# Two graph-attention layers on one core: the first pairs and the last pairs in another order, and one wait of VectorE per scores group in place of four

## The chip, the cores and the metric

The kernel runs on one core of a Trainium2 chip. Its engines are TensorE (PE, matrix products into PSUM), VectorE (DVE), ScalarE (ACT), GpSimd (POOL) and SyncE (SP, which here issues all DMAs). Each works through its own list of instructions in order, and they meet through semaphores. The metric is the device time of one execution in microseconds (us). Before the change it was 2106.66 us, the median of three runs (2102.52, 2106.66 and 2108.08).

## What is computed

128 graphs of 128 nodes with 384 features pass through two attention layers with 12 heads of 32. Cut to what matters:

```python
# layer 0: queries and keys without bias, bias on v, an output projection
q, k, v = x @ Wq.T, x @ Wk.T, x @ Wv.T + bv            # split into 12 heads
s = einsum('bqhd,bkhd->bhqk', q, k) * 384 ** -0.5 + 2 * adj
p = softmax(where(any(s != 0, -1), s, -inf)); p = nan_to_num(p)
x = layernorm(x + (p @ v) @ Wo.T + bo)
# layer 1: biases on q, k and v, no output projection
q, k, v = x @ Wq + bq, x @ Wk + bk, x @ Wv + bv
s = q @ k.T / sqrt(32) + beta * adj
p = softmax(where(adj > 0, s, -9e15))
x = layernorm(x + p @ v)
```

All tensors are f32. The projections are made as three products of a high and a low part each.

## The kernel before

The 128 graphs are worked on in 64 pairs. The rows, queries and keys of a pair are made together (256 columns); scores, softmax, values and norms are made per graph, g = 0 or 1. A step has the form `step(layer, pair, g)`. For one graph and one layer the steps follow one another like this:

- PE `transpose_x` / `transpose_x1`, then ACT `high_xT` / `high_x1T` and DVE `low_xT` / `low_x1T` (L1147), which split the transposed rows in two parts.
- PE `project_qk` j = 0 to 5 (nine products of 256 columns each, L408 to L410) and `project_v` (nine of 384), each taken out of its PSUM bank by ACT `qk_out` (L761 to L765), DVE `values_out0` (L1202) or ACT `values_out1`.
- PE `scores` (L458): 12 heads into four banks, three heads to a bank. DVE `negate` (L1125): 12 instructions that add the adjacency, write the negated scores and their minimum. ACT `exps` (L807): 12 exponentials with their sums, in slices `exps(layer, pair, g, first, end)`.
- Layer 0: POOL `fold_scores0`, DVE `abs_max` and `inverse_sums0` (L1174 to L1213), POOL `normalise0` (L1515). Layer 1: DVE `inverse_sums1` (L1183).
- DVE `flip_probs` (L1141) transposes inside blocks of 32 into the tile `flip` (layer 0) or `stage` (layer 1). SP `spread_probs` (L292) moves the blocks by four DMAs into `prob0T` or `prob1T`, which PE `attend` (L474) multiplies with the values.
- Layer 0: ACT `high_o0T`, DVE `low_o0T` (L1147), PE `project_out0`, DVE `add_residual0` (L1093), norm. Layer 1: ACT `out1T_out`, PE `transpose_out1`, DVE `attention_out1` (L1191), POOL `residual1` (L1507), norm, SP `store` (L260).

There is one tile for the probabilities of a layer, so the exponentials of a layer's next graph wait for the flip of the one before (`flip_done`), and a flip waits until the blocks of the one before have landed (`probT_loaded`). The sums of layer 1 stand in one tile too: its exponentials also wait for `inverse_sums1` of the graph before (`inv1_done`). `attention_out1(q, g)` waits for the store of the pair before with the same g, since both use y. Four PSUM banks go round among all other products (`RING_USERS`), so that a step often waits for the reader of an unrelated one.

Each engine's order is written out by hand. `iterations` (L98) runs `first()`, then `body` for pairs 3 to 7, then a loop over pairs 8 to 61 with two bodies in a turn, then `last()`. In one body five or six pairs are under way at different stages. In `first()` the pairs are called q0, q1, q2, ... from the start; in `last()` z0 is the last pair, z1 the one before it, and so on.

## Time and profile before

| | us |
|---|---|
| median of three runs | 2106.66 |
| the profiled execution, its own time | 2102.98 |
| its span, from the first to the last instruction | 2101.1 |
| PE busy | 2033.8 (97%) |
| ACT busy | 1884.3 (90%) |
| DVE busy | 1813.3 (86%) |
| POOL busy | 1644.0 (78%) |

The profile shows one execution on the chip. PE, DVE, ACT and POOL are the engines, PEld is PE's loading of weights, SPq is SyncE's issue of DMAs. A row of the timeline has the start in us from the span's start, the duration in us, engine, line and operation, output<-input, how many were merged, and, in brackets, how long the engine was idle before it and what released it. The granted clock of PE (PEclk) is a share of 2.4 GHz: 1.00 is 2.4 GHz, 0.50 is 1.2 GHz.

### The profile page before, as it was taken

The page shows a single profiled execution, that of the slowest core. Times are in us where ns is not written, and L with a number is a line of the kernel's source. Part 1 is how long each engine was busy: PE and PEld are TensorE (multiplying, and loading weights), DVE is VectorE, ACT ScalarE, POOL GpSimd, SP SyncE. Part 2 cuts the span into 40 slices and gives each one's busy share as a digit, 9 for nine tenths or more (in the row PEclk, how much of TensorE's full clock was granted, in tenths as well). Part 3 has the DMA queues.
Part 4 walks back from the last instruction along what each step waited for, and adds up shares of the span by engine and source line. Part 5 has one row for each costly group of instructions (what it writes and reads, how often), then busy time and mean ns, then how long its engine had stood idle before and what let it go on. Part 6 is the DMA issues. An engine that isn't in the chain of part 4 may idle for free.

```text
span 2101.1 us, 85420 instructions
## 1 busy us (share of the span) xinstructions
PE 2033.8 (97%) x23808; PEld 1910.1 (91%) x23808; DVE 1813.3 (86%) x8324; ACT 1884.3 (90%) x7816; POOL 1644.0 (78%) x2187
## 2 busy tenths in 40 slices
PE   6899999999999999999999999999999999999984
PEld 5799989999999999999999999999999999999974
DVE  4688889988989989888889888889889889888885
ACT  4699989999999999999999999999999999999885
POOL 3677878888888888888888888888888888788874
PEclk9999999999999999999999999999999999999997
DMA  4345555555555555555555555555555555555554
GB/s 147 73 107 134 136 134 127 140 134 125 141 134 126 140 134 128 138 134 129 137 134 129 137 134 131 135 134 132 134 134 136 130 134 136 130 134 137 122 125 109
DMA packets 225441, 274.22 MB, mean 131 GB/s; under 512 B 25680, under 2 KB 225360, under 8 KB 225360
## 3 DMA queue, kind: packets, MB, share of 16 engines
q1 hardware_dynamic: 225360, 273.26, 54.2%
q8 instruction: 36, 0.59, 0.1%
q14 instruction: 45, 0.37, 0.1%
HBM read 46.67 MB, written 25.17 MB: 34 GB/s over the span
## 4 chain that ended last, share of the span: by engine, by line
POOL 56%; issue 27%; PE 5%; POOLq 3%; DVE 3%; DMA 3%; SPq 2%; ACT 1%; DVEq 0%; ACTq 0%
POOL prob L1515 12%; POOL flip L1488 10%; POOL norm L1449 6%; POOL x_late L1500 5%; POOL y L1507 4%; POOL x_bo L1465 4%; POOL adj L1478 4%; POOL mask L1476 3%; POOL flip L1491 3%; POOL norm L1446 2%; DMA prob0T<-flip 2%; SPq L292 2%; POOL norm L1453 1%; PE r_bank L408 1%; PE r_bank L409 1%
## 5 line engine op out<-in xcount | busy, mean ns | idle before, releaser
L807 ACT ACTIVATE prob<-neg_s,heads 128x128 f32<-128x128 f32 x3072 | 1190.7, 393 | 17.7 <-DVE flip L1141 7.9
L807 ACT ACTIVATION_READ_ACCUMULATOR prob<-neg_s,heads 128x1 f32 x3072 | 591.6, 193 | 0.0
L1515 POOL TENSOR_TENSOR prob<-prob,heads 128x512 f32<-128x512 f32 x384 | 389.2, 1042 | 92.4 <-DVE heads L1213 92.4
L408 PE MATMUL r_bank<-xT_hi,w_hi 128*128 128x256 f32 x1152 | 356.4, 309 | 16.0 <-DVE xT_lo L1147 9.7
L1488 POOL TENSOR_TENSOR flip<-neg_s 128x768 f32<-128x768 f32 x128 | 236.0, 1843 | 169.1 <-DMA prob0T<-flip 161.5
L1125 DVE CUSTOM_DVE_ANT_0 neg_s<-s_bank,bias 128x128 f32<-128x128 f32 x1536 | 333.5, 286 | 18.9 <-PE s_bank L458 12.1
L1125 DVE CUSTOM_DVE_ANT_0 neg_s<-s_bank,adj 128x128 f32<-128x128 f32 x1536 | 333.5, 285 | 6.8 <-PE s_bank L458 6.7
L408 PE MATMUL r_bank<-x1T_hi,w_hi 128*128 128x256 f32 x1152 | 330.3, 287 | 3.5 <-DVE x1T_lo L1147 1.6
L410 PE MATMUL r_bank<-xT_hi,w_lo 128*128 128x256 f32 x1152 | 327.0, 284 | 0.0
L409 PE MATMUL r_bank<-xT_lo,w_hi 128*128 128x256 f32 x1152 | 326.8, 284 | 0.0
L409 PE MATMUL r_bank<-x1T_lo,w_hi 128*128 128x256 f32 x1152 | 324.2, 281 | 0.0
L410 PE MATMUL r_bank<-x1T_hi,w_lo 128*128 128x256 f32 x1152 | 323.8, 281 | 0.0
L408 PEld LDWEIGHTS r_bank<-xT_hi,w_hi 128*128 128x128 f32 x1152 | 218.8, 190 | 44.4 <-DVE xT_lo L1147 10.3
L1125 DVE DVE_READ_ACCUMULATOR2_ANT heads<- 128x1 f32 x3072 | 255.3, 83 | 0.0
L1141 DVE STREAM_TRANSPOSE flip<-prob 128x1536 f32<-128x1536 f32 x128 | 227.6, 1778 | 31.9 <-POOL prob L1515 30.4
L1141 DVE STREAM_TRANSPOSE stage<-prob 128x1536 f32<-128x1536 f32 x128 | 225.6, 1762 | 3.1 <-DMA prob1T<-stage 2.6
L408 PEld LDWEIGHTS r_bank<-x1T_hi,w_hi 128*128 128x128 f32 x1152 | 217.0, 188 | 5.5 <-issue 2.0
L409 PEld LDWEIGHTS r_bank<-xT_lo,w_hi 128*128 128x128 f32 x1152 | 219.9, 191 | 0.0
L410 PEld LDWEIGHTS r_bank<-xT_hi,w_lo 128*128 128x128 f32 x1152 | 219.3, 190 | 0.0
L409 PEld LDWEIGHTS r_bank<-x1T_lo,w_hi 128*128 128x128 f32 x1152 | 217.2, 189 | 0.0
L410 PEld LDWEIGHTS r_bank<-x1T_hi,w_lo 128*128 128x128 f32 x1152 | 216.7, 188 | 0.0
L1449 POOL TENSOR_TENSOR norm<-norm,neg_half 128x1 f32<-128x1 f32 x256 | 144.1, 563 | 21.3
(85 smaller groups left out, 5472.2 us busy)
## 6 DMA issues: line engine op xcount, KB each, us to landing
prob0T<-flip SPq DMA_DIRECT2D x512, 192.0 KB, 3.6
prob1T<-stage SPq DMA_DIRECT2D x512, 192.0 KB, 3.6
x_in<-in_x_dram SPq DMA_DIRECT2D x128, 192.0 KB, 3.3
out_dram<-y SPq DMA_DIRECT2D x128, 192.0 KB, 2.7
adj<-in_adj_dram SPq DMA_DIRECT2D x256, 64.0 KB, 2.7
prob<-in_L_gnn_Wq_dram SPq DMA_DIRECT2D x1, 576.0 KB, 4.5
prob0T<-in_L_gnn_Wk_dram SPq DMA_DIRECT2D x1, 576.0 KB, 5.7
stage<-in_L_gnn_Wv_dram SPq DMA_DIRECT2D x1, 576.0 KB, 7.8
```

Of the source, the lines that this page charges most:

```text
L408: pe.matmul(dst, a_hi(c), b_hi(c), start=(c == 0), stop=False)
L409: pe.matmul(dst, a_hi(c), b_lo(c), start=False, stop=False)
L410: mm = pe.matmul(dst, a_lo(c), b_hi(c), start=False, stop=(c == C - 1))
L807: act.activation(prob[layer][:, h, :], neg_s[layer][:, h, :], ACT.Exp, bias=neg_max[layer][:, h:h + 1], scale=-1.0, accum_out=row_sum[laye ...
L1125: dve.tensor_tensor_reduce(neg_s[layer][:, h, :], s_bank[b][:, (h // HC) * N:(h // HC + 1) * N], (adj0, bias1)[layer][q.parity][:, g, :], ...
L1141: dve.transpose(flip[layer].rearrange("p (j h b) -> p h j b", j=NB, h=H), prob[layer][:].rearrange("p h (j a) -> p h j a", j=NB)).then_inc ...
L1449: pool.tensor_tensor(rstd[layer][g][:], var_eps[layer][g][:], neg_half[:], ALU.pow).then_inc(rstd_steps[layer], 1)
L1465: pool.tensor_tensor(x_bo[b][:, g, :], x_in[b][:, g, :], bo_row[:], ALU.add).then_inc(x_bo_done, 1)
L1478: pool.tensor_scalar(adj1[:, g, :], adj1[:, g, :], 0.0, beta_col[:], ALU.max, ALU.mult).then_inc(bias1_steps, 1)
L1488: pool.tensor_tensor(fold_a, neg_s[0][:, :, 0:N // 2], neg_s[0][:, :, N // 2:N], ALU.add).then_inc(fold_steps, 1)
L1500: pool.tensor_tensor(x1_late[q.parity][:, g, :], x1[q.parity][:, g, :], bv_row[1][:], ALU.add).then_inc(late_done, 1)
L1515: pool.tensor_tensor(prob[0][:, hs, :], prob[0][:, hs, :], inv_sum0[:, hs].unsqueeze(2).to_broadcast([P, HC, N]), ALU.mult).then_inc(probn ...
```

## The change

The change has two parts. Nothing is computed otherwise than before.

The first part is one signal and one wait per scores group. PE raised `s_done` on each of the last four of the twelve head products, one for each bank, and DVE waited once for each bank. Now PE raises it on the last product alone, and DVE waits once ahead of the twelve instructions. ACT's `qk_out` waits for the same point as before.

```diff
@@ scores
-                        if c == C - 1:
-                            mm.then_inc(s_done[layer], 1)
+                    mm.then_inc(s_done[layer], 1)
@@ qk_out
-                    act.wait_ge(s_done[layer], q.plus(-2).count(HC, 1, HC))
+                    act.wait_ge(s_done[layer], q.plus(-2).count(1, 1, 1))
@@ negate
                             dve.wait_ge(exp_done[layer], q.count(H, g, 0))
-                        dve.wait_ge(s_done[layer], q.count(HC, g, b + 1))
-                        dve.sem_inc(dve_passed, 1)
+                            dve.wait_ge(s_done[layer], q.count(1, g, 1))
+                            dve.sem_inc(dve_passed, 1)
```

The second part is the order in `first()` and in `last()` on all five engines. `body`, and with it pairs 3 to 7 and the loop, keeps its order on each engine. A few of the lines:

```diff
@@ first, SP
+                load_adj0(q1)
                 load_x(q1)
-                load_adj0(q1)
+                load_adj1(q0)
@@ first, ACT
                 high_weights(WK0)
-                high_weights(WV0)
                 qk_out(0, q0, 0, 0)
+                high_weights(WO0)
@@ first, DVE
                 values_out0(q0, 0)
-                low_weights(WO0)
@@ last, PE
-                scores(1, z1, 1, LOOP_N)
                 project_qk(1, z0, 0, LOOP_N)
                 project_qk(1, z0, 1, LOOP_N)
-                transpose_out1(z2, 0, LOOP_N)
                 project_qk(1, z0, 2, LOOP_N)
+                scores(1, z1, 1, LOOP_N)
@@ last, SP
+                spread_probs(1, z2, 0)
                 store(z4, 1)
-                spread_probs(1, z2, 0)
+                store(z3, 0)
                 spread_probs(1, z2, 1)
-                store(z3, 0)
                 load_adj1(z0)
+                store(z3, 1)
                 spread_probs(1, z1, 0)
-                store(z3, 1)
                 store(z2, 0)
...
```

In DVE's part the line numbers are lower by five in the changed kernel (L1147 becomes L1142, L1141 becomes L1136).

The first place is DVE at the start of the program, right behind the twelve `negate` instructions of q0's graph 0. Before, the rows are these:

```order
L1202 TENSOR_TENSOR v_0<-r_bank,bv_row 128x384
L1084 TENSOR_TENSOR w_lo<-stage,w_hi 128x1152
L1202 TENSOR_TENSOR v_0<-r_bank,bv_row 128x384
L1174 TENSOR_REDUCE heads<-flip 128x12
L1176 SCALAR_TENSOR_TENSOR heads<-heads 128x12
L1209 RECIPROCAL heads<-heads 128x12
L1213 SCALAR_TENSOR_TENSOR heads<-heads 128x12
L1125 ISA neg_s,heads<-s_bank,adj_0 128x128
L1125 ISA heads 128x1
```

The same place in the changed kernel:

```order
L1197 TENSOR_TENSOR v_0<-r_bank,bv_row 128x384 x2
L1169 TENSOR_REDUCE heads<-flip 128x12
L1171 SCALAR_TENSOR_TENSOR heads<-heads 128x12
L1204 RECIPROCAL heads<-heads 128x12
L1208 SCALAR_TENSOR_TENSOR heads<-heads 128x12
L1142 TENSOR_TENSOR xT_lo<-r_bank,xT_hi 128x3x128 x2
L1136 STREAM_TRANSPOSE flip<-prob 128x12x4x32
L1120 ISA neg_s,heads<-s_bank,adj_0 128x128
L1120 ISA heads 128x1
```

The low part of the weight WO0 (L1084) has gone to a later place. The two low parts of q1's rows and the flip of q0's graph 0, which stood behind the twelve `negate` instructions of graph 1, stand ahead of them.

The second place is DVE in `last()`, around layer 1's graph 0 of z3. Before, these rows follow the flip of that graph, one L1191 and the twelve instructions of graph 1's `negate`, of which the last is the first row here:

```order
L1125 ISA heads 128x1
L1174 TENSOR_REDUCE heads<-flip 128x12
L1176 SCALAR_TENSOR_TENSOR heads<-heads 128x12
L1209 RECIPROCAL heads<-heads 128x12
L1213 SCALAR_TENSOR_TENSOR heads<-heads 128x12
L1147 TENSOR_TENSOR o0T_lo<-r_bank,o0T_hi 128x384
L1183 RECIPROCAL heads<-heads 128x12
L1103 BN_STATS norm_0<-y_0 128x6
```

In the changed kernel the flip itself (`stage<-prob`) is the second row, and the `negate` of graph 1 begins with the last:

```order
L1186 TENSOR_TENSOR y_0<-r_bank,heads 128x384
L1136 STREAM_TRANSPOSE stage<-prob 128x12x4x32
L1178 RECIPROCAL heads<-heads 128x12
L1088 TENSOR_TENSOR y_0<-r_bank,x_bo 128x384
L1098 BN_STATS norm_0<-y_0 128x6
L1101 BN_AGGR norm_0<-norm_0 128x2
L1120 ISA neg_s,heads<-s_bank,bias_0 128x128
```

Layer 1's reciprocal (L1183, now L1178) has moved from behind `negate`, the four instructions of layer 0's sums and a low part to the place right behind its flip.

The third place is SP near the end. `prob1T<-stage` is a spread of layer 1, `out_dram<-y_0` and `out_dram<-y_1` are stores of a graph 0 and a graph 1. Before, from the spread of z0's layer 0 graph 1 on (the x8 are both graphs of z2, the stores behind them are z3's graph 0, z3's graph 1 and z2's graph 0):

```order
L292 DMA prob0T<-flip 128x1x384 x4
L260 DMA out_dram<-y_1 32x4x384
L292 DMA prob1T<-stage 128x1x384 x8
L260 DMA out_dram<-y_0 32x4x384
L254 DMA adj<-in_adj_dram 128x1x128 x2
L292 DMA prob1T<-stage 128x1x384 x4
L260 DMA out_dram<-y_1 32x4x384
L260 DMA out_dram<-y_0 32x4x384
L292 DMA prob1T<-stage 128x1x384 x4
```

The same stretch in the changed kernel:

```order
L292 DMA prob0T<-flip 128x1x384 x4
L292 DMA prob1T<-stage 128x1x384 x4
L260 DMA out_dram<-y_1 32x4x384
L260 DMA out_dram<-y_0 32x4x384
L292 DMA prob1T<-stage 128x1x384 x4
L254 DMA adj<-in_adj_dram 128x1x128 x2
L260 DMA out_dram<-y_1 32x4x384
L292 DMA prob1T<-stage 128x1x384 x4
L260 DMA out_dram<-y_0 32x4x384
L292 DMA prob1T<-stage 128x1x384 x4
```

The stores of z3 each stand one spread earlier: graph 0's ahead of the spread of z2's graph 1, and graph 1's ahead of the spread of z1's graph 0.

## Rows read from the trace of the kernel before

**Rows 1.** Busy time by stretch (stretch: length, busy us per engine, PEclk, DMA share, GB/s).

```profile
0.00:30.00 30.00, 16.64 (x132) 14.61 (x132) 13.79 (x47) 15.17 (x39) 6.28 (x12) 1.00 0.60 193
30.00:40.00 10.00, 4.56 (x21) 4.59 (x22) 4.18 (x17) 2.75 (x12) 5.46 (x7) 0.54 0.50 117
40.00:110.00 70.00, 60.52 (x616) 55.32 (x615) 40.48 (x178) 43.70 (x168) 45.38 (x46) 0.99 0.28 66
110.00:300.00 190.00, 187.07 (x2193) 175.40 (x2192) 165.16 (x773) 172.21 (x727) 146.83 (x193) 1.00 0.55 127
300.00:1900.00 1600.00, 1600.00 (x18890) 1510.82 (x18890) 1437.34 (x6622) 1488.76 (x6212) 1299.88 (x1733) 1.00 0.56 134
1900.00:2000.00 100.00, 97.10 (x1168) 90.72 (x1166) 86.37 (x398) 89.76 (x377) 81.57 (x107) 1.00 0.52 123
2000.00:2101.00 101.00, 67.89 (x798) 58.68 (x798) 66.03 (x296) 71.92 (x289) 58.56 (x96) 0.86 0.50 121
```

**Rows 2.** Timeline of PE in the loop, scores groups.

```profile
612.79 0.95 PE L458 MATMUL s_bank<-k0T,q0T 32*128 32x128 f32 x24
622.45 0.95 PE L458 MATMUL s_bank<-k1T,q1T 32*128 32x128 f32 x24
644.23 0.95 PE L458 MATMUL s_bank<-k0T,q0T 32*128 32x128 f32 x24
```

**Rows 3.** Timeline of DVE in the loop, the first `negate` instruction of a group.

```profile
623.57 0.29 DVE L1125 CUSTOM_DVE_ANT_0 neg_s<-s_bank,bias 128x128 f32<-128x128 f32 x1 [0.16 <-PE s_bank L458]
```

**Rows 4.** Timeline of DVE at the start: a weight's low part, then three flips.

```profile
23.60 2.74 DVE L1084 TENSOR_TENSOR w_lo<-stage,w_hi 128x1152 fp32r<-128x1152 f32 x1
31.58 1.78 DVE L1141 STREAM_TRANSPOSE flip<-prob 128x1536 f32<-128x1536 f32 x1 [0.18 <-POOL prob L1515]
48.85 1.78 DVE L1141 STREAM_TRANSPOSE flip<-prob 128x1536 f32<-128x1536 f32 x1 [1.62 <-POOL prob L1515]
94.25 1.78 DVE L1141 STREAM_TRANSPOSE flip<-prob 128x1536 f32<-128x1536 f32 x1
```

**Rows 5.** Timeline of PE at the start, q1's first product.

```profile
35.44 0.55 PE L408 MATMUL r_bank<-xT_hi,w_hi 128*128 128x256 f32 x1 [6.65 <-DVE xT_lo L1147]
```

**Rows 6.** The page's groups: operation, count | busy us, mean ns | idle.

```profile
L807 ACT ACTIVATE prob<-neg_s,heads 128x128 f32<-128x128 f32 x3072 | 1190.7, 393 | 17.7 <-DVE flip L1141 7.9
```

**Rows 7.** Timeline of DVE and ACT in `last()`, around z3.

```profile
2006.18 1.77 DVE L1141 STREAM_TRANSPOSE stage<-prob 128x1536 f32<-128x1536 f32 x1
...
2013.83 0.22 DVE L1183 RECIPROCAL heads<-heads 128x12 f32<-128x12 f32 x1
...
2014.13 0.40 ACT L807 ACTIVATE prob<-neg_s,heads 128x128 f32<-128x128 f32 x1 [2.41 <-DVE heads L1183]
```

**Rows 8.** Timeline of DVE near the end: L1141 flips, L1191 readings of attended values.

```profile
2047.29 1.78 DVE L1141 STREAM_TRANSPOSE stage<-prob 128x1536 f32<-128x1536 f32 x1 [0.66 <-DMA prob1T<-stage]
...
2056.65 0.56 DVE L1191 TENSOR_TENSOR y<-r_bank,heads 128x384 f32<-128x384 f32 x1 [4.05 <-DMA out_dram<-y]
...
2065.88 0.56 DVE L1191 TENSOR_TENSOR y<-r_bank,heads 128x384 f32<-128x384 f32 x1 [3.60 <-DMA out_dram<-y]
2066.35 1.77 DVE L1141 STREAM_TRANSPOSE stage<-prob 128x1536 f32<-128x1536 f32 x1
...
2075.03 1.78 DVE L1141 STREAM_TRANSPOSE stage<-prob 128x1536 f32<-128x1536 f32 x1 [0.38 <-ACT prob L807]
...
2082.63 1.78 DVE L1141 STREAM_TRANSPOSE stage<-prob 128x1536 f32<-128x1536 f32 x1 [1.92 <-DMA prob1T<-stage]
```

**Rows 9.** Timeline of SP near the end: spreads and stores.

```profile
2058.92 3.07 SPq L292 DMA_DIRECT2D prob1T<-stage  x4
2062.04 3.91 SPq L260 DMA_DIRECT2D out_dram<-y  x2
...
2076.84 2.90 SPq L292 DMA_DIRECT2D prob1T<-stage  x4
```

**Rows 10.** Timeline of ACT near the end, z0's first exponential of layer 1.

```profile
2070.27 0.40 ACT L807 ACTIVATE prob<-neg_s,heads 128x128 f32<-128x128 f32 x1 [1.72 <-DVE heads L1125]
```

**Rows 11.** Timeline of PE, the last two attends.

```profile
2082.66 1.50 PE L474 MATMUL r_bank<-prob1T,v 128*32 128x128 f32 x24 [4.07 <-DMA prob1T<-stage]
...
2090.43 1.50 PE L474 MATMUL r_bank<-prob1T,v 128*32 128x128 f32 x24 [4.70 <-DMA prob1T<-stage]
```

More of the change, by code:

```diff
@@ L637, in last @@
-                scores(1, z3, 0, LOOP_N)
-                transpose_x1(z2, 0, LOOP_N)
-                project_v(1, z3, 1, LOOP_N)
-                project_v(0, z0, 1, LOOP_N)
-                project_qk(0, z0, 4, LOOP_N)
+                transpose_x1(z2, 1, LOOP_N)
                 project_qk(0, z0, 5, LOOP_N)
-                transpose_x1(z2, 1, LOOP_N)
+                attend(0, z1, 0, LOOP_N)
                 attend(1, z4, 0, LOOP_N)
-                attend(0, z1, 0, LOOP_N)
+                scores(0, z0, 0, LOOP_N)
@@ L663, in last @@
-                attend(1, z3, 0, LOOP_N)
                 project_v(1, z2, 1, LOOP_N)
                 transpose_x1(z1, 0, LOOP_N)
+                scores(1, z2, 0, LOOP_N)
                 transpose_x1(z1, 1, LOOP_N)
                 attend(0, z0, 0, LOOP_N)
-                scores(1, z2, 1, LOOP_N)
+                attend(1, z3, 0, LOOP_N)
+                transpose_out1(z3, 0, LOOP_N)
+                project_out0(z0, 0, LOOP_N)
                 project_qk(1, z1, 0, LOOP_N)
-                project_out0(z0, 0, LOOP_N)
@@ L1018, in last @@
[L1018 removed]
+                high_o0T(z0, 0)
+                out1T_out(z3, 0)
                 exps(0, z0, 1, 10, 12)
[L1020 to L1024 removed]
+                exps(1, z2, 0, 0, 8)
                 qk_out(1, z1, 0, LOOP_N)
[L1026 removed]
                 qk_out(1, z1, 1, LOOP_N)
+                exps(1, z2, 0, 8, 12)
@@ L1581, in last @@
                 inverse_std(0, z2, 1)
+                fold_scores0(z1, 1)
+                inverse_std(1, z5, 0)
+                normalise0(z1, 1)
+                inverse_std(1, z5, 1)
                 make_bias1(z3, 1)
-                fold_scores0(z1, 1)
-                late_x1(z3, 0)
-                normalise0(z1, 1)
-                inverse_std(1, z5, 0)
-                inverse_std(1, z5, 1)
+                residual1(z4, 0)
+                late_x1(z3, 1)
+                inverse_std(1, z4, 0)
```

452 lines of the change are left out of this document (223 added, 229 removed).

## The prediction

> **What bounds the kernel now.** I read the busy time by stretch first. The reader is to see one number in each row, the length less PE's busy time: 13.4 us without work in the first 30, then 5.4, 9.5 and 2.9 up to 300; 0 in the 1600 us from 300 to 1900; 2.9 and 33.1 in the last two stretches [rows 1]. Between 300 and 1900 PE is busy throughout at 2.4 GHz and a pair returns after 644.23 - 612.79 = 31.44 us [rows 2]. `body` keeps its order, so nothing is to be won there unless PE's own work shrinks, and the change moves no product. Only the 31.2 us of PE's idle time at the start and the 36.0 at the end are open. In both, PE is not what binds. There are two chains of VectorE, ScalarE, GpSimd and the spreads, one per layer: exponentials, flip, spread, next flip. I read these from the flips [rows 4, 8].
>
> **One wait per scores group.** The group that starts at 622.45 lasts 0.95, to 623.40, and the first `negate` instruction, which waited for the first bank alone, starts at 623.57, that is 0.17 after the whole group's end [rows 2, 3]. If the first bank had been handed over at three quarters of the group, it would have started 0.24 earlier. So the four banks come nearly together, and a wait for the last costs about 0. Bounds: above, 0.24 for each of some 8 groups at the end whose `negate` is on the chain, 1.9 us; below, 0, because in the loop nobody waits for VectorE (PE is never idle), and queued behind the wait are only the twelve instructions that need the banks anyway. I take 0, the value the start at 623.57 is nearest to.
>
> The Trainium skill (TensorE: Matmul & The Clock Gate, "The cost: per-tile semaphore tail") states that signals raised by many small products serialize at about 26 ns each and that one on the last is sound. By that rule three fewer would let VectorE start 0.08 earlier, 0.6 us over the same 8 groups, and the sum below would be 8.3 in place of 7.7. No run here shows the signal times yet, and the sum goes without it.
>
> **The start.** Before, q1's first product waits 6.65 us, to 35.44, for the low parts of q1's rows [rows 5]. These stood behind the low part of WO0 (2.74), graph 1's `negate` and the flip at 31.58 [rows 4]. None of them is needed. Now the low parts stand ahead of the flip, in the time in which VectorE waited for it, and PE can begin near 30, some 5.5 earlier. The long pause had also lowered the clock: 0.54 granted from 30 to 40, 21 matmuls in 4.56 us, 0.22 each [rows 1]. At 2.4 GHz they take half, which is another 2 to 3 us.
>
> This lead of 7 to 8 us isn't kept, because the layer-0 chain doesn't follow. Its flips start at 31.58, 48.85 and, three flips on, 94.25 [rows 4]: one interval of 17.3, then 45.40 / 3 = 15.1 each. The loop needs a flip of this layer each 31.44 / 2 = 15.7. So from the second flip on the start already runs at the loop's pace and PE soon waits for the attended values; what counts is how much earlier the second flip comes. At best its interval becomes 15.1 too, 2.2 less. But now the last four exponentials of q0's graph 1 stand behind the high part of the attended values of graph 0, which needs a whole spread, and behind the high weight of WV1. At worst ScalarE, which now waits for WO0's load between the first two outputs of q0, sets the start back; the outputs come one projection apart, nine products of 0.11 at 2.4 GHz, so about 1.0. Range -1.0 to 2.2; I take 1.3. The rest of the start is hidden by the chain. On SP q1's adjacency goes ahead of its rows (two DMAs, hidden: both have 20 us until use).
>
> **The end, around z3.** Layer 1's flip of graph 0 ends at 2006.18 + 1.77 = 2007.95. The exponentials of graph 1 start at 2014.13, after ScalarE sat idle for 2.41, released by the reciprocal at 2013.83 [rows 7]. The reciprocal stood behind twelve `negate` instructions, the four of layer 0's sums, for which VectorE needs layer 0's last exponential, and a low part. Now it stands right behind its flip. What is late next is that layer-0 graph's own normalisation on GpSimd, from which `residual1(z4, 0)` is taken away too. ScalarE is the busiest engine of this stretch besides PE, so 2.41 us of its idle time is worth 2.4. Bounds: 0 if the next wait takes it all; 4.3 if I follow each engine's new list from one step to the next up to the flip at 2047.29, which leaves out every collision. I take 2.4, the one length that a row shows.
>
> **The end, the last four flips.** They start at 2047.29 (z2, graph 1), then z1: 0.47 behind 2056.65, which is 2057.12 (the same 0.47 as from 2065.88 to 2066.35), and 2066.35; z0: 2075.03 and 2082.63 [rows 8]. Two of them stand behind an L1191 that waited 4.05 and 3.60 for a DMA of the output [rows 8]: the store of z3's graph 0 or 1, since SP issues it behind a spread, as the one at 2062.04 behind the spread at 2058.92 [rows 9]. Now each store stands one spread earlier. Followed from 2047.29:
> - Its end is 2049.07. Twelve exponentials at 0.393 [rows 6] are 4.7; among them stand one output and two high parts, about 0.5 each. z1's first flip can start at 2055.5, 1.6 earlier.
> - A flip must wait for the blocks of the one before: 2075.03 + 1.78 = 2076.81, next flip 2082.63, released by the DMA: 5.82 [rows 8]. So a round is at least 1.78 + 5.82 = 7.6: 2063.1, 2070.7, 2078.3.
> - For 2070.7, z0's exponentials must begin by 2066.0 in place of 2070.27 [rows 10]. The spread of z1's graph 0 has landed at 2057.3 + 5.8 = 2063.1; an attend and a scores group of 0.95 each at most, and the `negate` start of 0.5, give 2065.5. It holds.
>
> The last flip comes 4.3 earlier; with 0.1 for each of three handovers I take 4.0. Bounds: 1.6 (the first stall alone) to 4.3. All behind it, the attend at 2090.43 [rows 11] and the last norm and store, moves along. Store z3/1 now stands ahead of a spread and waits for a norm that ScalarE makes behind three outputs of z0: 2055.0 + 3 x 0.5 + 0.7 = 2057.2, about when the flip ends; up to 0.3 if late. The scores of z1's graph 1, now three projections (27 products of 0.11, 3.0 us) later, are needed only after that flip.
>
> **Sum.** 1.3 + 0 + 2.4 + 4.0 = 7.7 us, from the profiled execution's 2102.98 to 2095.3. The median of the three runs lies 3.7 above this execution, so the forecast is 2099.0, 0.36% less.
>
> **The rivals.**
> - **Eaten up.** The start gives nothing and at the end only one of the stalls goes, because the hand-made order meets other waits (four banks shared by all products, one tile per layer). For it: 5.5 us at the start are lost again by my own working; 33.1 us of idle PE show how tight the end is. Against: both L1191 waits and the 2.41 have a named cause that the new order removes. Price: -2.5, thus 2104.2.
> - **The clock.** The new order places pauses of PE anew; if those ahead of the projections of z1 and z0 let the clock fall to 1.2 GHz, as the 6.65 us did, each product costs 0.11 more: 2 x 54 of them are 11.9 us, all on the way to the last scores, and 27 at the start 3.0. With 7.7 gained that is +7.2, 2113.9. It decides once both sets run at half clock; with the set of z0 alone (5.9) it is still a gain of 1.8, or less by what the start loses. For it: mean clock 0.86 after 2000 [rows 1], and the attends of the last 20 us take 1.50 each [rows 11]. Against: those last attends lie behind all projections, and at the start the new order shortens the pause that cost the clock.
> - **The wait reaches the loop.** If the banks came a quarter group apart and PE waited for each, 54 x 4 x 0.24 = 51.8 us, 2158. Rows 3 and a PE without idle time speak against it.
> - **The longer lead holds.** 2.2 + 4.3 + 4.3 = 10.8, 2095.9. It is the far end of the forecast's own case.
>
> **How the numbers follow.** The forecast's case, a gain of 3 to 12 us, has 0.60; eaten up 0.31; the clock 0.08; the wait 0.01. A measurement of this kernel can tell 0.3%, 6.3 us, from no change. Of the forecast's case 0.50 lies beyond that and 0.10 within, of eaten up 0.03 beyond: faster 0.53, same 0.38, slower 0.09. The range goes from 2093 (the longer lead, and 3 us for the runs' own spread) to 2108 (the eaten-up case with the same).
>
> **What would show it.** Right: a pair still 31.44 in the loop, `negate` starting 0.2 behind the group; q1's first product near 30 and no 1.2 GHz behind it, yet the flip near 94 only 1 to 2 us earlier; no L1191 (now L1186) released by a DMA of the output near the end; last flips 7.6 to 7.8 apart. Wrong: a loop above 31.5; a second flip not before 48.5; z0's exponentials starting less than 3 us earlier, counted from the flip of z2's graph 1; a clock under 0.6 in the stretch of z0's projections.

## The result and the profile after

The change made the kernel slower: 2112.44 us median (21 runs, 2106.61 to 2121.41) against 2106.66 (21 runs, 2102.52 to 2110.72) of the kernel before, ratio 1.0027, 95% interval 1.0019 to 1.0035. The forecast was 2099.0, range 2093 to 2108. The profiled execution took 2111.26, span 2109.4.

Busy time by stretch, after (columns as in [rows 1]):

```profile
0.00:30.00 30.00, 16.93 (x132) 15.06 (x132) 11.60 (x37) 15.55 (x40) 9.30 (x14) 1.00 0.61 197
30.00:40.00 10.00, 9.78 (x72) 9.52 (x72) 6.19 (x28) 5.97 (x22) 2.13 (x3) 1.00 0.43 98
40.00:110.00 70.00, 55.52 (x548) 49.86 (x548) 39.92 (x175) 39.00 (x152) 43.00 (x45) 0.93 0.28 66
...
300.00:1900.00 1600.00, 1598.90 (x18921) 1509.84 (x18914) 1435.67 (x6610) 1488.80 (x6205) 1297.95 (x1732) 1.00 0.56 133
1900.00:2000.00 100.00, 95.72 (x1123) 90.15 (x1123) 87.03 (x408) 89.03 (x370) 79.72 (x104) 1.00 0.52 126
2000.00:2101.00 101.00, 72.73 (x865) 63.50 (x864) 67.40 (x297) 74.67 (x307) 60.35 (x96) 0.87 0.50 119
```

From 30 to 40 TensorE now works without a break at 2.4 GHz, as forecast, and gives it back from 40 to 110: idle 14.5 in place of 9.5, with a granted clock of 0.93 in place of 0.99 [rows 1]. The loop keeps its 31.44 a pair.

TensorE's and VectorE's timelines of the start, after (start, length, engine, line; in brackets the idle time before and what ended it), answering [rows 4, 5]:

```profile
30.23 0.36 PE L408 MATMUL r_bank<-xT_hi,w_hi 128*128 128x256 f32 x1 [0.59 <-DVE xT_lo L1142]
45.42 0.36 PE L408 MATMUL r_bank<-xT_hi,w_hi 128*128 128x256 f32 x1 [2.91 <-DVE xT_lo L1142]
53.69 0.69 PE L408 MATMUL r_bank<-w_hi,o0T_hi 128*128 128x384 f32 x1 [3.01 <-ACT q0T L760]
```
```profile
32.16 1.78 DVE L1136 STREAM_TRANSPOSE flip<-prob 128x1536 f32<-128x1536 f32 x1 [2.09 <-POOL prob L1510]
47.96 1.78 DVE L1136 STREAM_TRANSPOSE flip<-prob 128x1536 f32<-128x1536 f32 x1 [2.68 <-POOL prob L1510]
```

q1's first product comes at 30.23, and the second flip 0.89 earlier than before. But the fifth (95.69) comes 1.44 later, where the forecast had it 1 to 2 earlier.

VectorE near the end, after (L1136 flips, L1186 attention outputs), answering [rows 7, 8]:

```profile
2010.16 0.56 DVE L1186 TENSOR_TENSOR y<-r_bank,heads 128x384 f32<-128x384 f32 x1 [1.76 <-DMA out_dram<-y]
2010.64 1.77 DVE L1136 STREAM_TRANSPOSE stage<-prob 128x1536 f32<-128x1536 f32 x1
2012.33 0.19 DVE L1178 RECIPROCAL heads<-heads 128x12 f32<-128x12 f32 x1
...
2024.53 1.78 DVE L1136 STREAM_TRANSPOSE flip<-prob 128x1536 f32<-128x1536 f32 x1 [1.84 <-POOL prob L1510]
...
2053.50 0.56 DVE L1186 TENSOR_TENSOR y<-r_bank,heads 128x384 f32<-128x384 f32 x1 [1.96 <-DMA out_dram<-y]
2056.15 1.78 DVE L1136 STREAM_TRANSPOSE stage<-prob 128x1536 f32<-128x1536 f32 x1
...
2065.06 1.78 DVE L1136 STREAM_TRANSPOSE stage<-prob 128x1536 f32<-128x1536 f32 x1 [2.34 <-ACT prob L806]
...
2073.41 1.78 DVE L1136 STREAM_TRANSPOSE stage<-prob 128x1536 f32<-128x1536 f32 x1 [0.68 <-DMA prob1T<-stage]
2080.84 0.56 DVE L1186 TENSOR_TENSOR y<-r_bank,heads 128x384 f32<-128x384 f32 x1 [2.68 <-PE r_bank L485]
2081.31 1.77 DVE L1136 STREAM_TRANSPOSE stage<-prob 128x1536 f32<-128x1536 f32 x1
...
2090.68 1.78 DVE L1136 STREAM_TRANSPOSE stage<-prob 128x1536 f32<-128x1536 f32 x1 [2.12 <-DMA prob1T<-stage]
```

The two waits of 4.05 and 3.60 for an output DMA are gone, though an attention output near them still waits 1.96 for one (2053.50), and another 1.76 (2010.16); the last four flips are 8.91, 8.35, 7.90 and 9.37 apart, 34.53 in all against 35.34 before and 31.0 forecast. And the flip they start from is itself 8.86 later than in the first profile of the kernel before.

TensorE near the end, after:

```profile
2028.97 1.18 PE L458 MATMUL s_bank<-k1T,q1T 32*128 32x128 f32 x24 [4.31 <-DVE heads L1120]
...
2078.30 1.66 PE L458 MATMUL s_bank<-k1T,q1T 32*128 32x128 f32 x24 [3.10 <-DVE heads L1120]
```

Two scores groups now stand waiting for `negate` instructions to free the banks; the longest such pause near the end was 1.72 before (at 2051.81).

### The profile page after: what moved, and what is told of

The parts are those of the page before. It is cut to its first block, busy times and chain, and to the rows that moved or that the text cites. A ratio compares the mean times of both kernels' runs of the same rounds, so it can differ in the third digit from the quotient of the medians.

```text
span 2109.4 us, 83789 instructions
## 1 busy us (share of the span) xinstructions
PE 2036.9 (97%) x23808; PEld 1913.5 (91%) x23808; DVE 1812.8 (86%) x8324; ACT 1885.8 (89%) x7816; POOL 1640.7 (78%) x2187
## 4 chain that ended last, share of the span: by engine, by line
PE 87%; DMA 3%; POOL 2%; issue 2%; SPq 2%; DVE 2%; ACT 0%; POOLq 0%; DVEq 0%; ACTq 0%
PE r_bank L408 22%; PE r_bank L409 21%; PE r_bank L410 21%; PE s_bank L458 10%; PE r_bank L473 8%; DMA prob0T<-flip 3%; PE r_bank L391 2%; PE r_bank L485 2%; PE r_bank L401 2%; SPq L292 2%; DVE flip L1136 1%; POOL prob L1510 1%; POOL flip L1483 1%; POOL flip L1486 0%; DVE neg_s L1120 0%
## 5 line engine op out<-in xcount | busy, mean ns | idle before, releaser
L1136 DVE STREAM_TRANSPOSE flip<-prob 128x1536 f32<-128x1536 f32 x128 | 227.6, 1778 | 27.7 <-POOL prob L1510 25.6
L1136 DVE STREAM_TRANSPOSE stage<-prob 128x1536 f32<-128x1536 f32 x128 | 225.5, 1762 | 5.2 <-DMA prob1T<-stage 2.8
```

The source lines that it names most:

```text
L1136: dve.transpose(flip[layer].rearrange("p (j h b) -> p h j b", j=NB, h=H), prob[layer][:].rearrange("p h (j a) -> p h j a", j=NB)).then_inc ...
```

## The experiments

Each kernel was timed in five rounds beside the kernel before on the same chip; ratios are to it, with their 95% intervals.

| kernel | median us | ratio |
|---|---|---|
| changed | 2112.44 | 1.0027 (1.0019 to 1.0035) |
| e1 single wait alone | 2110.07 | 1.0014 (1.0005 to 1.0023) |
| e2 + new start | 2110.40 | 1.0013 (1.0004 to 1.0022) |
| e3 + new end | 2112.99 | 1.0026 (1.0016 to 1.0036) |
| e4 changed, old waits | 2109.05 | 1.0012 (1.0003 to 1.0021) |
| e5 four waits, one signal, +77 | 2114.31 | 1.0033 (1.0021 to 1.0045) |
| e6 before, +74 | 2108.95 | 1.0008 (0.9999 to 1.0017) |
| e7 single wait, +130 | 2116.86 | 1.0045 (1.0033 to 1.0057) |
| e8 single wait, 3 a body | 2110.01 | 1.0012 (1.0003 to 1.0021) |
| e9 changed, 3 a body | 2114.78 | 1.0027 (1.0017 to 1.0037) |
| e10 new SyncE list alone | 2120.57 | 1.0062 (1.0048 to 1.0076) |
| e11 early reciprocal | 2108.18 | 1.0005 (0.9996 to 1.0014) |
| e12 two stores earlier | 2104.19 | 0.9988 (0.9979 to 0.9997) |
| e13 e4, negate ahead | 2108.53 | 1.0013 (1.0004 to 1.0023) |
| e14 one signal, old lists | 2108.14 | 1.0006 (0.9997 to 1.0015) |
| e15 3 a body, in a gap | 2107.32 | 1.0005 (0.9996 to 1.0014) |
| e16 e12 + e11 | 2103.90 | 0.9989 (0.9980 to 0.9998) |
| e17 e12 + new start | 2103.25 | 0.9984 (0.9976 to 0.9993) |

**How far one profile carries.** 

> The kernel before, unchanged, profiled once more, since its first profile (2102.98) lies at the fast end of its runs (median 2107.6). If its layer-0 flips in the loop stand 2 to 3 us later than in that first profile, 1 of it between 290 and 411, this much of what the changed kernel seemed to lose at the start and in the loop is the spread of runs. If they stand within 0.5, the loss there belongs to the change.

This execution of the unchanged kernel took 2110.51. Its fifth layer-0 flip comes at 96.66 (+2.41), the one near 411 +3.63, the last flip at 2090.36 (+7.73): later by nearly as much as in the changed kernel (+8.05). The execution profiled first was one of the shortest of its kernel, and differences of a few us between two profiles say nothing here. From here on the medians decide, and of profiles only intervals within one are used. Even these are not all steady: from VectorE's first layer-1 flip behind the loop to its last flip the two profiles of the same kernel take 125.88 and 129.67.

**The change in four parts.** e1 is the kernel before with this alone:

```diff
-                        if c == C - 1:
-                            mm.then_inc(s_done[layer], 1)
+                    mm.then_inc(s_done[layer], 1)
...
-                        dve.wait_ge(s_done[layer], q.count(HC, g, b + 1))
-                        dve.sem_inc(dve_passed, 1)
+                            dve.wait_ge(s_done[layer], q.count(1, g, 1))
+                            dve.sem_inc(dve_passed, 1)
```

e2 adds all five lists of `first()` to e1, e3 in their place those of `last()`; e4 is the changed kernel with the removed lines back.

> The kernel before with the one change that TensorE signals once per scores group and VectorE waits once. Theory A (the new order behind the loop loses the time): this edit costs nothing, ratio 1.000 within 0.001, the pair in the loop 31.44 us, the first negate instruction 0.17 to 0.35 behind its group. Rival W (the single wait costs at the two ends, where VectorE is on the chain, 0.2 for each of some 20 groups): +2 to +4 us, ratio 1.001 to 1.002, and the layer-0 flips of the start already 1 us late.

> The kernel after with the order behind the loop as before (single wait, new order of the first five bodies). Theory A: the new start costs about 1 us (its flips stood +1.1 to +1.4 late from the fourth on), so ratio 1.0003 to 1.001, the flip near 94.25 at 95 to 96, the last flip 1 to 3 us late. Rival S (the start loses the whole difference, since from the flip near 317 on it was 3.5 us late): +4 to +6 us, ratio 1.002 to 1.003, and again a spread that lands late near 313.

> The kernel after with the order of the first five bodies as before (single wait, new order behind the loop). Theory A: the end loses 4 to 5 us, ratio 1.0019 to 1.0024, with the last attend 4 to 5 us later, counted from the layer-1 flip near 1959. Rival S: +0 to +1 us. Rival C (the pauses of TensorE lower its clock at the end in some executions): the runs of this kernel spread over 10 us or more as those of the changed kernel did, the longer ones with the lower mean granted clock, while the kernel with the new start alone spreads no more than the kernel before.

> The kernel after with the four signals and four waits per scores group of the kernel before, the orders new. Theory A: no difference from the changed kernel, ratio 1.002 to 1.003 to the kernel before. Rival W: the wait was the loss, ratio 1.000 to 1.001, and the negate instructions of the end start about 0.2 us earlier behind their groups.

The single wait costs 0.14% alone and 0.15% on top of the new orders (1.0027 less 1.0012): about 3 us. Theory A, by which it cost nothing, fell with that. The start shows nothing (1.0013 against 1.0014, 1.0027 against 1.0026). The order behind the loop costs 0.12 to 0.14%, 2.7 us. Rival S fell.

In the profiles the new start wins and loses again, in each of the six kernels that have it (changed, e2, e4, e9, e13, e17). From the first layer-0 flip to the second it takes 15.4 to 15.9, the old start 16.1 to 17.5. From the third to the fourth it takes 16.2 to 18.2, the old start 14.9 to 15.1. VectorE's list has the reason: the new one has the `negate` of q2's graph 0 ahead of the flip of q1's graph 1, the fourth, and the old one behind it. In the changed kernel:

```profile
77.47 0.29 DVE L1120 CUSTOM_DVE_ANT_0 neg_s<-s_bank,adj 128x128 f32<-128x128 f32 x1 [1.04 <-PE s_bank L458]
...
80.01 1.77 DVE L1136 STREAM_TRANSPOSE flip<-prob 128x1536 f32<-128x1536 f32 x1
```

GpSimd had finished what this flip needs at 79.08. In the six kernels the flip starts 0.9 to 2.4 behind GpSimd's end, right behind the `negate`, which had waited 1.0 to 2.5 for the scores. With the old start VectorE waits for GpSimd (1.73) and flips at once.

The loss behind the loop can be placed too. I compare the stretch from VectorE's first layer-1 flip there to z2's second, like with like. With four waits it is 90.5 and 93.6 in the two profiles of the kernel before, 93.1 and 96.0 with the new order (e4, e13). With the single wait it is 95.4 and 94.6 (e1, e2), and 96.3 and 98.1 with the new order (changed, e3). The last four rounds, behind that flip, take 32.8 to 34.6 in these four kernels with the new order, 35.3 to 36.4 in those with the old one. So the new order loses ahead of z2's second flip and gains behind it.

Rival C fell too: e3's nine runs lie within 3.2, the new start's within 7.

**A stall that the single wait moves.** In e1 the layer-0 flips from 1954.46 to 1972.77 are 18.31 apart; before it was 1968.19 less 1952.26, 15.93. VectorE's timeline in e1, and of the kernel before at its nearest like row ("issue": it waited for nothing that the profile shows):

```profile
1970.52 0.56 DVE L1146 TENSOR_TENSOR o0T_lo<-r_bank,o0T_hi 128x384 fp32r<-128x384 f32 x1 [2.63 <-issue]
```
```profile
1979.40 0.29 DVE L1125 CUSTOM_DVE_ANT_0 neg_s<-s_bank,bias 128x128 f32<-128x128 f32 x1 [1.75 <-issue]
```

In e1 TensorE then waits for this low part (0.66, at 1971.13), the flip comes late, and TensorE waits for its spread. e7 (below) has the stall at the same place. Both at the same product of the list, e1 first:

```profile
1981.53 1.51 PE L473 MATMUL r_bank<-prob0T,v 128*32 128x128 f32 x24 [2.12 <-DMA prob0T<-flip]
```
```profile
1987.88 0.86 PE L473 MATMUL r_bank<-prob0T,v 128*32 128x128 f32 x24 [2.06 <-DMA prob0T<-flip]
```

Before, this wait was 0.66 (at 1976.93). In e1 and e2 the granted clock is 0.5 for 3.4 us behind the wait, in e7 it stays 1.0: from the first layer-1 flip behind the loop to z2's second e1 takes 95.4, e7 91.1, no longer than the kernel before. So one profile with the stall at this place shows no loss at z2's second flip, and what the stall costs is not the same in each execution.

In both places the stop goes with one packet on a DMA queue that the profile calls "instruction". The DMA view of e1 from 1968 to 1970 shows it, and the changed kernel's page has such queues over the whole span (packets, MB, share):

```profile
q14 instruction: 1, 0.01, 1.7%
```
```profile
q8 instruction: 36, 0.59, 0.1%
q14 instruction: 44, 0.36, 0.1%
```

0.36 MB in 44 packets is 8.2 KB each. The Trainium skill (Runtime: NRT & Kernel Launch, "Instruction fetch mechanics") has instructions come in blocks of 16 KiB, 256 instructions, and the crossing of a border mostly hidden; by that size a packet of q14 is 128 instructions, an estimate. Here the packets of q14 are half of the skill's block, those of q8 are 16 KB, and the crossing behind the loop was not hidden. I counted where in VectorE's list the stall stands. The next kernels moved it: e5 and e6 with increments at VectorE's very start, where it waits for loads,

```diff
             def first():
+                for _ in range(77):    # e5; 74 in e6, 130 in e7
+                    dve.sem_inc(dve_passed, 1)
```

> The kernel before with TensorE signalling once per scores group, but VectorE keeping a wait ahead of each bank's negate instructions (all four now on the one signal), and 77 semaphore increments at VectorE's very start, where it waits for loads. By their number VectorE's instruction list stands 77 instructions past its loop's end where in the kernel before it stalled for 1.75 with nothing to wait for (row 1979.40, released by issue). Theory P (the single wait costs by the place of that stall, which it moves ahead of the low part of layer 0's attended values): ratio 1.000 within 0.001, the stall again in the middle of the negate instructions of z4's graph 1. Rival W (one signal for four hands the banks over later): ratio 1.0014, as with the single wait, wherever the stall is. The Trainium skill (Runtime: NRT & Kernel Launch, Instruction fetch mechanics) has the instructions come in blocks of 256; by it the first block border past the loop would be where each kernel stalls, and a shift by so many instructions moves the stall by as many.

> The kernel before with its four signals and four waits, and 74 semaphore increments at VectorE's very start. They put the instruction at which VectorE stalls 3 instructions past its loop's end, where the kernel with the single wait has it. Theory P: the stall moves from 1979 to near 1970, ahead of the low part of layer 0's attended values, the layer-0 flip of 1968.19 comes 1.5 to 2.5 late against the flip before it, ratio 1.0007 to 1.0014. Rival W: ratio 1.000 within 0.0005, the flip in its place. Rival N (the increments themselves delay the start): the first negate instruction, 20.9 to 22 before, is over 0.5 late.

> The kernel with the single signal and wait, orders as before, and 130 semaphore increments at VectorE's very start, so that the stall lands 129 instructions past the loop's end, near the low part of z2's transposed rows, for which VectorE waited 1.76 for ScalarE anyway (row 1994.16). Theory P: no stall near 1970, ratio 0.999 to 1.0003, 2 to 3 us less than with the single wait alone. Rival W: 1.0014 as without the increments. Rival N: the first scores group over 0.5 late.

My count was wrong, and with it what theory P expected of e5 and e7 (1.000, measured 1.0033 and 1.0045): increments ahead of the loop didn't move the stall (e6: again in the middle of `negate`, at 1985.10; e7: again ahead of o0T_lo). They made another one. VectorE in e6 and in e7, at the loop's first return:

```profile
270.54 0.56 DVE L1147 TENSOR_TENSOR x1T_lo<-r_bank,x1T_hi 128x384 fp32r<-128x384 f32 x1 [3.04 <-issue]
```
```profile
273.98 0.56 DVE L1146 TENSOR_TENSOR x1T_lo<-r_bank,x1T_hi 128x384 fp32r<-128x384 f32 x1 [3.04 <-issue]
```

From the flip near 220 to the one near 411 these kernels take 194.0 to 194.6, all others 191.6 to 193.3: 1.7 us. That is as much as e6's 0.08%. In e7 TensorE also begins 5.6 later, since 130 increments take longer than the loads. e5 keeps 0.25% beyond the 1.7 us, more than the single wait costs. Its stall falls in layer 0's `negate`; why it costs so much is open.

e5's stall, at 1992.63, gave the rule. It stands 108 instructions past the loop's end where the loop has 407, 77 past it where it has 438 (the kernel before), 4 past it where it has 383 (the single wait): 128 times 4, 4 and 3, plus 3, counted from the loop's start (407 and 108 as 438 and 77 make 515, 383 and 4 make 387; the count is good to an instruction or two). So three increments at the end of each body in the loop:

```diff
                 low_xT(p2, 0)
+                if not isinstance(r, int):
+                    for _ in range(3):
+                        dve.sem_inc(dve_passed, 1)
```

> The kernel before with the single signal and wait, and three semaphore increments at the end of each of the two bodies in VectorE's loop (six in the loop's list, none outside it). In the runs so far the stall behind the loop stood 77 instructions past the loop's end where the loop had 438 instructions, 4 past it where it had 383 (whatever stood ahead of the loop), 108 past it where it had 407: each is 128 times a whole number, plus 3, counted from the loop's start. With 389 it should stand 126 past the end, near the low part of z2's transposed rows. Theory P (the single wait costs by shortening the loop so that the stall falls right behind it): no stall near 1970, a stall between 1992 and 2000, ratio 0.9995 to 1.0005. Rival W (one signal for four, or the single wait itself, costs): 1.0014 as without the increments. Rival B (any stall within 128 instructions behind the loop costs the same): stall moved, ratio still 1.0014.

> The changed kernel with the same three semaphore increments at the end of each of the two bodies in VectorE's loop. Theory P: the same 2 to 3 us come back, ratio 1.0010 to 1.0018 against 1.0027 without them, as with new orders and old wait (1.0012). Rivals W and B: 1.0027. All agree that the new order behind the loop keeps its own loss of 2 to 3 us.

The stall moved as computed (VectorE in e8):

```profile
1997.73 0.18 DVE L1105 BATCH_NORM_AGGREGATE norm<-norm 128x2 f32<-128x6 f32 x1 [3.76 <-issue]
```

The time did not follow (e8 1.0012 where theory P had 1.0005 at most, e9 1.0027 where it had 1.0018 at most), and rival B seemed right. But the loop had become longer: 1134.1 for 36 pairs against 1132.18 before, and as much in e9. Without these 1.9 us (0.09%) the two would stand at 1.0003 and 1.0018, an estimate. TensorE, never idle from 400 to 1900 before, lost 1.08 there, waiting for low parts behind the increments (busy by stretch, e8, then e15 below):

```profile
400.00:1900.00 1500.00, 1498.92 (x17719) 1414.83 (x17719) 1343.22 (x6201) 1394.92 (x5818) 1214.87 (x1625) 1.00 0.56 133
```
```profile
400.00:1900.00 1500.00, 1500.00 (x17723) 1415.79 (x17723) 1346.05 (x6212) 1396.25 (x5824) 1215.67 (x1624) 1.00 0.56 134
```

e15 has the same increments ahead of `abs_max(n, 0)`, where VectorE waits for GpSimd. e14 leaves VectorE's list as it was before and changes TensorE alone:

```diff
-                        if c == C - 1:
-                            mm.then_inc(s_done[layer], 1)
+                    mm.then_inc(s_done[layer], HC)
```

> The kernel with the single signal and wait, and the six increments in VectorE's loop moved from the end of each body to ahead of the folded maximum of graph 0, where VectorE waits 0.46 per pair for GpSimd. At the body's end they made the loop 1.9 us longer over 36 pairs (1134.1 against 1132.1), which was most of their 1.0012. Theory P: 36 pairs again in 1132.0 to 1132.6, the stall again near 1997, ratio 0.9998 to 1.0008. Rival B (a stall anywhere in the 128 instructions behind the loop costs the same): 1132 too, but ratio 1.0012 to 1.0016. Rival W: the same as B.

> The kernel before with one edit on TensorE alone: no signal from the last product of each bank, and one that counts four from the last product of the group. VectorE's and ScalarE's lists are those of the kernel before to the last instruction, waits and all. Rival W (what costs is that the first bank is handed over with the last): ratio 1.0014, as with the single wait. Theory P (what costs is VectorE's shorter list, whose stall behind the loop then falls elsewhere): the first negate instruction still starts 0.60 behind the start of the group's last product in place of 0.45, but ratio 0.9997 to 1.0005, and the stall again in the middle of the negate instructions of z4's graph 1.

e15: 1132.12 for 36 pairs, stall at 1994.66, ratio 1.0005, 0.09% under e1. e14: stall again in `negate` (1980.11), 1.0006. By the midpoints the place of the stall is worth about 1.8 us (1.0014 less 1.0005 or 1.0006), and about 1.2 (1.0005, 1.0006) is left for everything else. The intervals of e14 and e15 reach below 1.0, and both overlap that of e1. So the single wait's 3 us are measured, and their split is not: that the stall's place is the larger part is argued from midpoints, and e7's profile speaks against it.

The late hand-over shows in the loop. TensorE's group and VectorE's first `negate` in the changed kernel:

```profile
625.94 0.95 PE L458 MATMUL s_bank<-k1T,q1T 32*128 32x128 f32 x24
```
```profile
627.22 0.29 DVE L1120 CUSTOM_DVE_ANT_0 neg_s<-s_bank,bias 128x128 f32<-128x128 f32 x1 [0.53 <-PE s_bank L458]
```

1.28 behind the group's start, before 623.57 less 622.45, 1.12 [rows 2, 3]. Nearly all groups on which `negate` waited (48 to 59 in a trace) lie in the loop. Counted from the start of the group's last product, `negate` begins there at 0.446 with four signals. With the one signal of the changed kernel it begins at 0.50 and 0.60 by turns, from one pair to the next, whether one wait or four follow (e5). With e14's one signal that counts four it begins at 0.496 in every pair, where I had expected 0.60. So handing the first bank over with the last is 0.05 later; what adds another 0.10 in every other pair of the single-signal kernels was not found. The loop doesn't feel it. At the two ends VectorE waited for scores at five to seven groups, mostly 0.05 to 0.06 later than with four signals (0.614 to 0.629 against 0.565): some 0.4 us in all, an estimate.

**The order behind the loop.** e10 takes SyncE's new list alone; e11 moves one reciprocal, e12 two stores:

```diff
-                inverse_sums1(z3, 0)          # e11: out from behind low_o0T(z1, 1)
...
                 attention_out1(z4, 0)
+                inverse_sums1(z3, 0)
                 negate(1, z3, 1, (0, 1, 2, 3))
```
```diff
+                store(z3, 0)                  # e12
                 spread_probs(1, z2, 1)
-                store(z3, 0)
                 load_adj1(z0)
+                store(z3, 1)
                 spread_probs(1, z1, 0)
-                store(z3, 1)
```

> The kernel before with SyncE's list behind the loop taken from the changed kernel (each output store one spread earlier, the spreads and loads of adjacency as there) and nothing else. The prediction's step (the two flips near the end wait for a store issued behind a spread): no attention output of the last pairs is released by a DMA of the output near 2056 and 2066, last flip 1.6 to 4.0 earlier, ratio 0.9981 to 0.9993. Rival R (the spread is then late by the 0.6 of the store's issue and shares the DMA engines with it, and the next wait is close behind): the waits go, ratio 1.000 within 0.0005.

> The kernel before with one step of VectorE moved: the reciprocal of z3's graph 0 stands behind its attention output of z4 and ahead of the negate instructions, no longer behind twelve of them and a low part. The prediction's step: ScalarE's exponentials of z3's graph 1 no longer wait for it, 2.4 us (0 to 4.3) earlier from there on, ratio 0.9988. Rival E (the next wait takes it all: the attention output in between waits for a store, the exponentials for their negate instructions): those exponentials at most 0.5 earlier, ratio 1.000 within 0.0005.

> The kernel before with two steps of SyncE moved: store z3/0 ahead of the spread of z2's graph 1 and store z3/1 ahead of the spread of z1's graph 0, both behind norms that are long finished by then; nothing else. This is the prediction's step alone, without the store z4/0 that the whole new list put ahead of a norm not yet made. The prediction's step: no attention output released by a DMA of the output near 2056 and 2066, last four flips 7.6 to 8 apart, 1.6 to 4.0 gained, ratio 0.9981 to 0.9993. Rival R (the waits go, but the flips then wait for ScalarE's exponentials and for the spread before, which starts 0.6 later): rounds of 8.5 to 9.3, ratio 0.9995 to 1.0005.

e10 lost 13 us and tested something else: the new list also loads z2's adjacency four steps later, and GpSimd's old list needs it early (13.29 idle for that DMA at 2019.35, VectorE 13.27 behind it). A list of one engine isn't a part that can be tried alone.

e11: the wait of 2.41 is gone, and the next one is longer by as much. ScalarE's timeline before, and in e11:

```profile
2019.72 0.71 ACT L786 ACTIVATE x<-y,norm 128x384 f32<-128x384 f32 x1 [1.60 <-POOL norm L1453]
```
```profile
2021.34 0.71 ACT L786 ACTIVATE x<-y,norm 128x384 f32<-128x384 f32 x1 [4.16 <-POOL norm L1453]
```

1.60 and 2.41 are 4.01, and it waits 4.16 there now. Ratio 1.0005, from 0.9996: the 2.4 us (0.9988) are ruled out.

e12 is faster, 0.12% or 2.6 us. VectorE in e12:

```profile
2050.66 1.78 DVE L1141 STREAM_TRANSPOSE stage<-prob 128x1536 f32<-128x1536 f32 x1
2058.84 0.56 DVE L1191 TENSOR_TENSOR y<-r_bank,heads 128x384 f32<-128x384 f32 x1 [2.89 <-PE r_bank L486]
2059.79 1.78 DVE L1141 STREAM_TRANSPOSE stage<-prob 128x1536 f32<-128x1536 f32 x1 [0.38 <-ACT prob L807]
...
2083.52 1.78 DVE L1141 STREAM_TRANSPOSE stage<-prob 128x1536 f32<-128x1536 f32 x1 [1.97 <-DMA prob1T<-stage]
```

The four rounds take 9.13, 7.87, 8.22 and 7.64, 32.86 in place of 35.34. In the first of them the flip, no longer behind the output's DMA, is at once bound by ScalarE's exponentials, as rival R had it; the rest comes as forecast.

**The pause of TensorE.** e13 swaps `flip_probs(0, z0, 0)` and `negate(0, z0, 1, ...)` in e4.

> The changed kernel with four signals and waits as before (ratio 1.0012 so far), and in VectorE's list behind the loop the negate instructions of z0's graph 1 (layer 0) ahead of the flip of its graph 0, in place of behind it. Theory Z (the new order loses because TensorE stands 4.2 us at the scores of z2, which need the banks that these instructions free, while VectorE waits 1.8 for GpSimd at the flip; the pause also lowers the clock behind it to 0.5 to 0.8): the pause shrinks by 3 to 3.6 us, the granted clock from 2030 to 2040 is 1.00, ratio 0.9990 to 1.0003. Rival E (the next wait takes it): pause gone, ratio still 1.0008 to 1.0016.

TensorE in e4, then in e13:

```profile
2025.83 1.00 PE L458 MATMUL s_bank<-k1T,q1T 32*128 32x128 f32 x24 [4.24 <-DVE heads L1121]
```
```profile
2021.16 0.95 PE L458 MATMUL s_bank<-k1T,q1T 32*128 32x128 f32 x24 [0.98 <-DVE heads L1121]
2027.24 0.87 PE L401 MATMUL r_bank<-ident,x 128*128 128x128 f32 x3 [5.13 <-ACT x L786]
```

The pause only moved to z1's transposes, whose rows wait for a norm; the granted clock from 2030 to 2040 was 0.60, and the time stayed (1.0013 against e4's 1.0012). Theory Z fell, rival E held.

**The parts that pay, together.**

> The kernel before with the two output stores one spread earlier and the reciprocal of z3's graph 0 ahead of the negate instructions, everything else (four waits, start) as before. If the two add up as measured one by one (0.9988 and 1.0005, whose interval reaches down to 0.9996), ratio 0.9985 to 0.9995. If the reciprocal had been worth its 2.4 us and was only hidden by the waits for the stores, now gone, 0.9977 or less.

> The kernel before with the two output stores one spread earlier and the changed kernel's order of the first five bodies, four waits. The prediction's step for the start (a gain of 1.3) would give 0.9982. From the runs so far (the new start on top of the single wait: 1.0013 against 1.0014, and 1.0027 against 1.0026) the start is worth nothing: 0.9988, with the first flip about 0.6 earlier and the fifth about 1 later, counted from TensorE's first product.

e16 equals e12, and its interval ends above 0.9977: the reciprocal is worth nothing without the stores' waits too. e17 is the fastest kernel, 2103.25. Its distance to e12 (0.04%) is less than can be measured; 0.9984 lies between the 0.9988 of a start worth nothing and the 0.9982 of the forecast's 1.3, so that a small gain of the start is not ruled out.

## Why the prediction was wrong

The forecast was a gain of 7.7 us, the kernel lost 5.8. Three terms of the sum failed in their mechanism, one was too large, and the new order behind the loop has a cost for which the sum had no term.

**One wait per scores group (term 0, upper bound 1.9): wrong, about 3 us.** I reasoned that the four banks come nearly together, and they do: the products of the last four heads start 7 ns apart. The step that failed is "a wait for the last costs about 0". VectorE's first `negate` starts 0.05 us later with one signal at the end of the group (e14), and 0.10 more in every other pair with the changed kernel's signal. This makes some 0.4 us at the two ends. By the rule of the Trainium skill (TensorE: Matmul & The Clock Gate, "The cost: per-tile semaphore tail") I had VectorE start 0.08 earlier, an estimate. That rule is on the end of all signals, and the first `negate` waited for the first of four; the trace shows it 0.05 to 0.15 later. The rest was not in my sum at all. VectorE stands once behind the loop for "issue", and fewer instructions in the loop's list moved this stall from the middle of a `negate` to right behind the loop, ahead of a low part that TensorE waited for. By midpoints this is the larger part (1.8 of 3); it is argued, not shown. I had read VectorE's rows around 2047 and not the 1.75 at 1979.40.

**The start (1.3): about 0 (each contrast to 0.12%, so that 1.3 itself is not ruled out).** The forecast of the product near 30 and of the clock held, and the second flip came 0.9 earlier. The step that failed is that behind the second flip the start runs at the loop's pace whatever the order: the interval from the third flip to the fourth is 16.2 to 18.2 with the new start and 15.0 with the old one, because the fourth flip now stands behind a `negate` that waits for scores. The fifth flip came no earlier. I had looked at the steps ahead of the second flip alone. The changed kernel also has new waits of 2.91 and 3.01 at TensorE on the way.

**z3's stretch (2.4): 0.** The wait had a named cause and it went, but the step "2.41 us of its idle time is worth 2.4" failed: GpSimd's norm, for which ScalarE had waited 1.60, now kept it waiting 4.16 (e11). I had named GpSimd's part as next and not asked when it would be ready.

**The last four flips (4.0): 2.6 by the stores alone (e12), mis-sized.** z0's first exponential of layer 1 did begin 3.2 earlier, counted from z2's second flip (19.80 against 22.98). I took 8.2 for the first round and 7.6 for the others; e12 has 9.13, 7.87, 8.22 and 7.64, the changed kernel 8.91, 8.35, 7.90 and 9.37. Of the last one, z1's last attend stands behind the scores group that waits 3.10 at 2078.30, and the spread of z0's graph 0 is not issued before 2084.83, 1.75 behind its flip's end. But the wait alone does not do it. e3, with the same order, has the same wait:

```profile
2082.21 0.95 PE L458 MATMUL s_bank<-k1T,q1T 32*128 32x128 f32 x24 [3.10 <-DVE heads L1122]
```

The group takes 0.95 there, not 1.66, and the last round is 7.57. In the changed kernel, e4 and e9 the granted clock is 0.5 for 6.8 us from about this group on, over the nine products behind it, and the last round is 9.3 to 9.5; in e3 and e13 the clock stays 1.0 there, and it is 7.6 and 7.7.

**What is missing in the sum.** The new order behind the loop is 2.7 slower than the old one. If it still holds e12's 2.6, the rest of it loses about 5, an estimate; the sum had no term for it. This lies ahead of z2's second flip, where TensorE now pauses 4.31 at a scores group and the granted clock is 0.68 from 2030 to 2040. Taking that pause away gave nothing (e13). Which moves make up the 5 stays open.

Of the rivals, the clock (2113.9, 0.08) came nearest in time, and this was luck. The mean clock after 2000 is 0.86 before and 0.87 after, and near the end the clock fell to half over nine products of z0, not over both sets of projections. "Eaten up" described the start and z3 rightly and stopped at zero.

## What to carry over

Removing instructions from an engine's loop can have a price: read where the profile has that engine waiting for "issue" around the loop's ends, and compute where it will stand after the edit. For every wait that an edit removes, look up when the next thing in the list is ready; in a tail with four tight engines, moving only the transfer that others wait for (two stores) paid, and reordering all five lists lost it twice over. Profile the kernel before a second time: two executions of it lay 7.5 us apart, more than the 5.8 that were to be explained. When an interval differs in one profile, look for it in every kernel that shares the order: the last round of 9.37 comes only with the clock at half, and e3 shows it.

## What the hardware showed that was not expected

- One stall of VectorE behind the loop, with one packet of 8.2 KB on an instruction queue beside it: 1.3 to 4.0 us in every kernel run, at 128 times a whole number plus 3 instructions from the loop's start, to within an instruction or two, with loops of 383, 389, 407 and 438 instructions; what stands ahead of the loop had no influence. ScalarE has one of 1.1 to 2.2 behind the loop in most kernels, TensorE none over 1. At the loop's first return ScalarE stalls 2.4 to 3.2 in each kernel, VectorE 2.95 to 3.04 in e5, e6 and e7 only; why there was not found.
- A bank's own signal releases VectorE 0.05 earlier than one signal of the group that counts four (0.446 against 0.496), though the products of the last four heads start 7 ns apart; with one signal that counts one it is 0.05 and 0.15 by turns, unexplained.
- The same wait of 3.0 to 3.1 in the same order of products was followed by half clock in three kernels (changed, e4, e9) and by full clock in two (e3, e13), and the last round differs by 1.6 to 1.9 us.
- Three semaphore increments (some 0.1 us each: VectorE's first instruction starts at 13.35 behind e7's 130, at 8.44 behind e5's 77) at the wrong place of a body that has 3 us of idle time cost 0.05 us a pair.
